# Two tables per pick with shared compares, and one-sample dot products on quarters of the array

## The chip, the cores and the metric

The kernel runs on one core of a Trainium2 chip. The time is device microseconds from one launch. TensorE multiplies matrices, VectorE (DVE) and ScalarE (ACT) work element by element, GpSimd (POOL) gathers rows of memory by index, and SyncE (SP) starts transfers.

## The reference

A recommendation tower for a batch of 512. Each sample has 32 ids, one per embedding table; each table has rows of 128 floats (1,000 to 125,000 rows). The 32 rows of a sample are multiplied with each other, and the products of different rows (496 of them), with 16 dense values, go through three dense layers.

```python
e = stack([tbl_f[ids[:, f]] for f in range(32)], axis=1)      # 512 x 32 x 128
z = einsum('bnd,bmd->bnm', e, e)[:, iu, ju]                   # pairs n < m: 512 x 496
h = concatenate([z, dense_ctx], axis=1)                       # 512 x 512
h = maximum(h @ W_top1 + b_top1, 0)                           # 512 x 512
h = maximum(h @ W_top2 + b_top2, 0)                           # 512 x 256
y = h @ W_top3                                                # 512 x 1
```

All of it is in 32-bit floats.

## The kernel before

All 32 rows of a sample are brought into `emb`, 128 partitions (the embedding's elements) x 512 samples x 32 tables. Seventeen tables are **gathered**: GpSimd starts 68 indirect transfers (line 307), each of 128 rows, paced by the picks that are done (`pace`), and TensorE transposes what lands (`turn`, line 574), one to four tiles at a time; ScalarE copies the transposed tiles into `emb` (`emb_out`).

The fifteen smallest tables are **picked**: they are loaded whole, and TensorE multiplies the table by a matrix of zeros and ones. A table has 8 or 10 row blocks (`KR`). Eleven tables of 1,000 rows have 8, four of 1,250 rows have 10, 128 blocks in all, taken in the order of their size. For each block:

- an `onehot` tile (128 x 512) is made by comparing the table's 512 ids, which every partition holds (`pick_id`, 16 bits), with the number of the row that the partition has in this block (`own_row`). VectorE makes some directly in 32 bits (`make_onehots`, line 326); for the others it writes 16 bits (`narrow`, line 336), and ScalarE widens them, several blocks in one instruction (line 442). `BY_ACT` says how many of a table's blocks go that second way, 75 in all.
- the table is split so that two fast passes give the full precision: ScalarE rounds it (`high`, line 421), VectorE subtracts (`low`, line 316). TensorE then does two matmuls per block (lines 564 and 566) with the same `onehot`.

Three tables, four tables' ids and 16 `onehot` tiles are held at a time. SyncE loads the ids and rows of the next table when the buffers come free. VectorE's order is written out: in the loop of table t it waits for the ids of table t+1 and makes its narrow compares, then makes the `low` pieces and direct compares of table t by turns. The ids of table t+1 were asked for when VectorE had finished table t-3, so they are there long before. TensorE does `pick(t)` and then `turn(t-2)`. A pair of tables shares one tile of PSUM, which ScalarE copies into `emb` when both are done (`pick_out`; the last three alone, `pick_alone`).

Then come the **dot products** (`dot_pairs`, line 606). One matmul takes two samples, 64 columns against themselves, and writes a 64 x 64 block, of which the two 32 x 32 blocks on the diagonal are used. Even and odd matmuls go to the two halves of the array's columns (`tile_position`). Eight groups of 64 samples follow each other; ScalarE and VectorE copy half a group each to SBUF (line 196), 512 columns of which a half is used later. The blocks are stored to memory and loaded back in another order (`dots_store`, `pairs_load`), and go through the three layers (lines 625, 636, 641). The order on TensorE after the picks is written out: dots of groups 0 to 5, the last transposes, group 6, layer 1 of the first half of the batch, the rest of the dots, layers 2 and 3.

Of the kernel before, what the change touches and what calls it, by code (L numbers as in the profile page):

```python
# [19 lines left out]

PIECE = 2
PIECES0 = KR[0] // PIECE
LOW_CUT, HOT_CUT = [4, 4, 2], [3]
# [8 lines left out]

LOWS = [cut(KR[0], [PIECE])] + [cut(k, LOW_CUT) for k in KR[1:]]
LOW0 = [sum(len(p) for p in LOWS[:t]) for t in range(PICK + 1)]

BY_ACT = [2, 4, 5, 5, 5, 5, 5, 5, 5, 5, 5, 6, 6, 6, 6]

HALF1 = KR[1] // 2

TWOS = -(-PICK // 2)  # L40
ACT0 = [sum(BY_ACT[:t]) for t in range(PICK + 1)]

ACT_K0 = [KR[t] - BY_ACT[t] if t < 3 else 0 for t in range(PICK)]
DVE_K0 = [0 if t < 3 else BY_ACT[t] for t in range(PICK)]
# [14 lines left out]
LAG = 2  # L59
TABLES_HELD, IDS_HELD, HOT, ROWS_HELD = 3, 4, 16, 7  # L60
# [4 lines left out]
def pace(c):  # L65
    return min(51 * c // 20 - 10, CHUNK0[PICK])
# [13 lines left out]
def build(nc, row_ids, pick_ids, tables, lone, picked, context, w1, w2, small, y):  # L80
# [4 lines left out]
    with ctx:  # L85
# [6 lines left out]
        def sem(name):  # L92
# [10 lines left out]
        pick_id = sb("pick_id", [P, IDS_HELD, B], i16)  # L103
        home = sb("home", [P, 2, 2 * F, BLK // 4], f32)
        table = home[:, :, :, :].rearrange("p i c g -> p (i c g)")[:, 0:TABLES_HELD * KRMAX * D].rearrange(
            "p (t n) -> p t n", t=TABLES_HELD)
        high = sb("high", [P, TABLES_HELD, KRMAX * D], f32r)
        low = sb("low", [P, TABLES_HELD, KRMAX * D], f32r)
        onehot = sb("onehot", [P, HOT, B], f32r)
        narrow = sb("narrow", [P, 2, NARROW, B], mybir.dt.float16)  # L110


        dot_sb = home
        pairs = sb("pairs", [P, BLOCKS, 4, PC, BLK // 4], f32)
        w1_sb = sb("w1_sb", [P, PC, H1], f32)
        w2_sb = sb("w2_sb", [P, N1, H2], f32)
        small_sb = sb("small_sb", [P, N1 + 2 * N2], f32)
        h1 = sb("h1", [P, N1, B], f32)
        h2 = sb("h2", [P, N2, B], f32)
        y_row = sb("y_row", [1, B], f32)  # L120
# [9 lines left out]
        pick_ps = [two_ps[(TWOS - 1) % 2][:, i, :] for i in range(2)]  # L130
        dot_ps = [free_ps, [two_ps[TWOS % 2][:, i, :] for i in range(2)]]
# [14 lines left out]
        pick_ids_in = [sem(f"pick_ids_in{t}") for t in range(PICK)]  # L146
# [16 lines left out]
        picked_done = sem("picked_done")  # L163
        pick_emb_ready = sem("pick_emb_ready")
        turned = sem("turned")
# [19 lines left out]
        def by_dve(t):  # L185

            return CHUNK0[t] - ACT0[t]
# [5 lines left out]
        def copy_dots(copy, grp, j):  # L193

            at = GRP // 4 * (grp % 2) + GRP // 8 * j
            return copy(dot_sb[:, grp // 2 % 2, :, at:at + GRP // 8],  # L196
                        dot_ps[grp % 2][j][:, :].rearrange("p (g c) -> p c g", c=2 * F))

        def dots_store(queue, r, s):
            queue.dma_start(dot_out[r][s, 0:F * F, :].rearrange("(a j) g -> a j g", j=F),  # L200
                            dot_sb[32 * s:32 * s + 32, r % 2, F * (s % 2):F * (s % 2) + F, :]
                            ).then_inc(dots_stored[r], 16)
# [18 lines left out]
        def copy_last_dots(copy, half):  # L221
# [3 lines left out]
                        last_dot_ps[half][:, 0:B // 2].rearrange("p (g c) -> p c g", c=2 * F))  # L225
# [4 lines left out]
        def _(sp):  # L230
            def ids_load(t):
                if t >= IDS_HELD:
                    sp.wait_ge(onehot_dve, by_dve(t - IDS_HELD + 1))
                    sp.wait_ge(narrow_ready, ACT0[t - IDS_HELD + 1])
                sp.dma_start(pick_id[:, t % IDS_HELD, :], pick_ids[:, t, :]).then_inc(pick_ids_in[t], 16)

            def table_load(t):
                if t >= TABLES_HELD:
                    sp.wait_ge(low_ready, LOW0[t - TABLES_HELD + 1])
                sp.dma_start(table[:, t % TABLES_HELD, 0:width(t)],  # L240
# [6 lines left out]
            for j in range(PIECES0):  # L247
                sp.dma_start(table[:, 0, n * j:n * (j + 1)], first[:, n * j:n * (j + 1)]).then_inc(piece_in[j], 16)
            table_load(1)
            for t in range(2, PICK):  # L250
                ids_load(t)
                table_load(t)
# [60 lines left out]
        def _(dve):  # L313
            def split_low(t, a, b):
                at = t % TABLES_HELD
                dve.tensor_tensor(low[:, at, a:b], table[:, at, a:b], high[:, at, a:b],  # L316
                                  ALU.subtract).then_inc(low_ready, 1)

            def make_onehots(t, k0, k1):

                i = STEPS.index(KR[t])
                for k in range(k0, k1):
                    c = CHUNK0[t] + k
                    if c >= HOT:
                        dve.wait_ge(picked_done, c - HOT + 1)
                    dve.tensor_scalar(onehot[:, c % HOT, :], pick_id[:, t % IDS_HELD, :], own_row[:, i, k:k + 1], None,  # L326
                                      ALU.is_equal).then_inc(onehot_dve, 1)

            def make_narrow(t):

                i = STEPS.index(KR[t])
                if t >= 2:
                    dve.wait_ge(onehot_act, ACT0[t - 1])
                for n in range(BY_ACT[t]):
                    k = ACT_K0[t] + n
# [442 lines left out]
```

## Time and profile before

| | |
|---|---|
| Time, three runs | 124.79, 125.47, 125.48 us (median 125.47) |
| Profiled execution: span from first to last instruction | 148.7 us |
| The profiled execution's own time beside the span | none is given but the span |
| Busy share of the span: TensorE, VectorE, ScalarE, GpSimd | 82%, 51%, 53%, 48% |
| Mean granted clock of TensorE | 0.919 |
| Picks (lines 564 and 566) | 4.8 to 79.4 us of the span |
| Dot products (line 606) | 83.8 to 131.4 us |

"Busy" is the time in which an engine had an instruction under way. The profiled execution is 23.2 us longer than the median of the runs, so its rows give durations, and their sum is not the time. A record of TensorE is one pass of instructions as the hardware has them: a product of 32-bit floats shows as more than one record.

### The profile page before, as it was taken

What the parts mean: (1) busy time and instruction counts of PE and PEld (TensorE: products, weight loads), DVE (VectorE), ACT (ScalarE), POOL (GpSimd) and SP (SyncE); (2) the same over time, 40 slices, a digit from 0 to 9 for tenths busy, and PEclk for the clock granted to TensorE, in tenths of its full rate; (3) what the DMA queues carried; (4) which work ended last, traced back from release to release, by engine and by line L of the source; (5) the groups of instructions that cost most, each with busy time, mean ns of one, the idle gap of its engine ahead of it and who ended that gap; (6) DMA issues with size and microseconds to landing.
All of it is one profiled execution on the core that took longest, in us unless ns stands there. A gap on an engine that the chain in (4) does not pass through costs nothing.

```text
span 148.7 us, 2677 instructions
## 1 busy us (share of the span) xinstructions
PE 121.4 (82%) x1028; PEld 99.5 (67%) x1028; DVE 75.2 (51%) x196; ACT 78.8 (53%) x79; POOL 71.3 (48%) x76
## 2 busy tenths in 40 slices
PE   5889979989999689499995464321999899999993
PEld 3457758868788468378884452111999798999971
DVE  2999999989897399496800000000333033223301
ACT  3588899999997897799950510000143302210022
POOL 3877749787787477378775577772000000000000
PEclk9999999999999999959999776555599999999999
DMA  5998736666667356793221011211056441024000
GB/s 144 275 338 267 234 100 204 204 216 225 217 219 235 110 178 195 232 324 113 55 53 52 23 53 53 53 53 35 4 146 202 136 126 35 4 78 127 10 0 1
DMA packets 11150, 19.81 MB, mean 133 GB/s; under 512 B 2353, under 2 KB 7473, under 8 KB 11138
## 3 DMA queue, kind: packets, MB, share of 16 engines
q1 hardware_dynamic: 7522, 13.74, 29.8%
q0 software_dynamic: 2176, 4.46, 10.3%
q10 hardware_dynamic: 1440, 1.44, 3.0%
q8 instruction: 8, 0.13, 0.3%
q14 instruction: 4, 0.03, 0.1%
HBM read 17.54 MB, written 2.13 MB: 132 GB/s over the span
## 4 chain that ended last, share of the span: by engine, by line
PE 64%; ACT 15%; issue 11%; another core or an unknown queue 5%; DVE 2%; DMA 2%; ACTq 0%
PE two_ps L564 15%; PE two_ps L566 14%; PE two_ps L606 8%; PE two_ps L625 8%; ACT onehot L442 8%; PE free_ps L606 7%; ACT emb L421 5%; PE free_ps L636 3%; PE turn_ps L574 3%; PE two_ps L636 2%; ACT high L421 2%; DMA id_sb<-row_ids 2%; PE two_ps L641 1%; PE turn_ps L625 1%
## 5 line engine op out<-in xcount | busy, mean ns | idle before, releaser
L307 POOL DMA_INDIRECT rows<-tables,row_no x64 | 66.6, 1040 | 26.5 <-issue 14.9
L564 PE MATMUL two_ps<-onehot,high 128*128 128x512 f32 x128 | 52.7, 412 | 7.4 <-ACT onehot L442 4.3
L566 PE MATMUL two_ps<-onehot,low 128*128 128x512 f32 x128 | 50.9, 397 | 0.0
L442 ACT ACTIVATE onehot<-narrow 128x2560 fp32r<-128x2560 f16 (+3 forms) x16 | 35.5, 2226 | 4.8 <-PE two_ps L566 3.0
L564 PEld LDWEIGHTS two_ps<-onehot,high 128*128 128x128 f32 x128 | 24.8, 193 | 16.7 <-issue 10.4
L566 PEld LDWEIGHTS two_ps<-onehot,low 128*128 128x128 f32 x128 | 24.8, 194 | 4.7
L326 DVE TENSOR_SCALAR onehot<-pick_id,own_row 128x512 fp32r<-128x512 int16 x53 | 23.0, 479 | 4.4 <-PE two_ps L566 3.5
L316 DVE TENSOR_TENSOR low<-home,high 128x512 fp32r<-128x512 f32 (+1 forms) x36 | 22.4, 625 | 3.8 <-issue 3.7
L336 DVE TENSOR_SCALAR narrow<-pick_id,own_row 128x512 f16<-128x512 int16 x75 | 22.4, 365 | 0.0
L606 PE MATMUL two_ps<-emb 128*64 128x64 f32 x240 | 12.9, 247 | 9.4 <-issue 9.3
L196 DVE COPY home<-free_ps 128x512 f32<-128x512 f32 x4 | 2.8, 692 | 33.8 <-remote 29.8
L421 ACT ACTIVATE high<-home 128x1024 fp32r<-128x1024 f32 (+3 forms) x19 | 17.8, 941 | 2.5 <-DMA home<-picked 2.4
L606 PEld LDWEIGHTS two_ps<-emb 128*64 128x64 f32 x240 | 10.3, 158 | 11.6 <-issue 11.5
L421 ACT ACTIVATE emb<-turn_ps 128x512 f32<-128x512 f32 (+2 forms) x20 | 11.3, 574 | 10.9 <-PE turn_ps L574 7.2
L606 PE MATMUL free_ps<-emb 128*64 128x64 f32 x272 | 11.7, 251 | 5.6 <-ACT emb L421 4.5
L421 ACT ACTIVATE emb<-two_ps 128x1024 f32<-128x1024 f32 (+1 forms) x9 | 12.8, 1421 | 6.4 <-remote 6.4
L606 PEld LDWEIGHTS free_ps<-emb 128*64 128x64 f32 x272 | 10.8, 164 | 6.7 <-ACT emb L421 5.2
L625 PE MATMUL two_ps<-pairs,w_sb 128*128 128x128 f32 x104 | 12.6, 277 | 0.0
L625 PEld LDWEIGHTS two_ps<-pairs,w_sb 128*128 128x128 f32 x104 | 12.0, 192 | 0.1
L421 ACT ACTIVATE home<-two_ps 128x512 f32<-128x512 f32 x4 | 2.4, 596 | 17.8 <-PE two_ps L606 17.8
L340 DVE TENSOR_SCALAR h<-two_ps,small_sb 128x128 f32<-128x128 f32 x15 | 4.3, 346 | 13.1 <-PE two_ps L625 12.2
L574 PE MATMUL turn_ps<-ident,rows 128*128 128x128 f32 x64 | 9.9, 274 | 0.8 <-issue 0.8
(37 smaller groups left out, 54.5 us busy)
## 6 DMA issues: line engine op xcount, KB each, us to landing
home<-picked SPq DMA_DIRECT2D x10, 512.0 KB, 3.6
home<-picked SPq DMA_DIRECT2D x4, 640.0 KB
pick_id<-pick_ids SPq DMA_DIRECT2D x13, 128.0 KB, 3.7
w_sb<-w SPq DMA_DIRECT2D x3, 512.0 KB
dot_out<-home SPq DMA_DIRECT2D x10, 128.0 KB, 2.4
rows<-tables,row_no POOLq DMA_INDIRECT x64
dot_out<-home ACTq DMA_DIRECT2D x6, 128.0 KB, 2.6
pairs<-dot_out SPq DMA_DIRECT2D x10, 64.0 KB, 2.0
```

The lines of the kernel that those rows point to most:

```text
L307: pool.indirect_dma_start(rows[:, k % ROWS_HELD, i, :], None, lone if one_table else tables, bass.IndirectOffsetOnAxis(ap=id_sb[:, 0, c:c ...
L316: dve.tensor_tensor(low[:, at, a:b], table[:, at, a:b], high[:, at, a:b], ALU.subtract).then_inc(low_ready, 1)
L326: dve.tensor_scalar(onehot[:, c % HOT, :], pick_id[:, t % IDS_HELD, :], own_row[:, i, k:k + 1], None, ALU.is_equal).then_inc(onehot_dve, 1)
L336: dve.tensor_scalar(narrow[:, t % 2, n, :], pick_id[:, t % IDS_HELD, :], own_row[:, i, k:k + 1], None, ALU.is_equal).then_inc(narrow_ready, 1)
L421: return act.activation(out, in_, ACT.Copy)
L442: act.activation(onehot[:, at:at + n, :], narrow[:, t % 2, n0:n0 + n, :], ACT.Copy).then_inc(onehot_act, n)
L564: pe.matmul(out, high[:, at, D * k:D * (k + 1)], onehot[:, c % HOT, :], start=(k == 0), stop=False)
L566: pe.matmul(out, low[:, at, D * k:D * (k + 1)], onehot[:, c % HOT, :], start=False, stop=(k == KR[t] - 1)).then_inc(picked_done, 1)
L574: last = pe.transpose(turn_ps[k % 2][:, i * P:(i + 1) * P], rows[:, k % ROWS_HELD, i, :], ident[:, :])
L606: last = pe.matmul(out, e, e, start=True, stop=True, tile_position=(0, 64 * h))
L625: last = pe.matmul(h1_ps[r][n], w1_sb[:, c, n * P:(n + 1) * P], pairs[:, r:r + 1, :, c, :], start=(c == 0), stop=(c == PC - 1))
L636: return pe.matmul(h2_ps[part][n], w2_sb[:, c, n * P:(n + 1) * P], h1[:, c, samples(part)], start=(c == 0), stop=(c == N1 - 1))
```

## The change

It does two things. **Teams.** Tables 1 to 14 are picked in seven teams of two tables of equal size; table 0 is alone (`TEAMS`). One compare serves the same row block of both tables, on 2 x 512 ids, because both have the same `own_row` number; `onehot` and `narrow` tiles have room for two tables. There are 68 such steps instead of 128 blocks, 25 of them by way of ScalarE (`BY_ACT`). Two teams are held (`HELD`), their rows, `high`, `low`, ids and `narrow` tiles, and 8 double `onehot` tiles. TensorE does a step of both tables, four matmuls, then the next; a team is cut in two halves with a `turn` behind each. In the last team the first table's steps from `SPLIT` on go ahead of the second's, so that it can be copied out earlier, and the copy of the second table is shared by ScalarE and VectorE. The weights of layer 2, the hidden layers and the result use the memory of the ids and `narrow` tiles, so that load waits for the last compares.

**Dots of one sample.** A matmul takes one sample, 32 columns against themselves, and goes to one of the four quarters of the array's columns in turn. All that is written is used; the copies to SBUF have half the columns.

```diff
+TEAMS = [[0]] + [[t, t + 1] for t in range(1, PICK, 2)]
+BY_ACT = [2, 3, 3, 3, 3, 3, 4, 4]
+HELD, HOT, ROWS_HELD = 2, 8, 7
 # SyncE
-                sp.wait_ge(onehot_dve, by_dve(t - IDS_HELD + 1))      # IDS_HELD = 4, tables
-                sp.wait_ge(narrow_ready, ACT0[t - IDS_HELD + 1])
+                sp.wait_ge(onehot_dve, DVE0[g - HELD + 1])            # HELD = 2, teams
+                sp.wait_ge(narrow_ready, ACT0[g - HELD + 1])
+                ids_load(sp, g)
+                table_load(g, 0)
+                table_load(g, 1)
...
+            sp.wait_ge(onehot_dve, DVE0[NT])
+            sp.wait_ge(narrow_ready, ACT0[NT])
             sp.dma_start(w2_sb[:, :, :], w2.rearrange("(c p) n -> p c n", p=P)).then_inc(weights_in, 16)
 # VectorE
+                    dve.tensor_scalar(onehot[:, c % HOT, 0:n, :], pick_ids_of[:, g % HELD, 0:n, :],
+                                      own_row[:, STEPS.index(KT[g]), k:k + 1], None,
                                       ALU.is_equal).then_inc(onehot_dve, 1)
...
+            for g in range(1, NT):
+                if 1 < g < NT - 1:
+                    dve.wait_ge(pick_ids_in[g + 1], 16)
+                    make_narrow(g + 1)
+                if g >= HELD:
+                    dve.wait_ge(picked_done, STEP0[g - HELD + 1])
+                own = KT[g] - BY_ACT[g]
+                pieces = [(i, k0, k1) for k0, k1 in LOWS[g] for i in range(2)]
+                for j, (i, k0, k1) in enumerate(pieces):
+                    if k0 == 0:
+                        dve.wait_ge(high_ready, PIECES0 + 2 * (g - 1) + i + 1)
+                    split_low(g, i, k0, k1)
+                    if j:
+                        n = len(pieces) - 1
+                        make_onehots(g, DVE_K0[g] + own * (j - 1) // n, DVE_K0[g] + own * j // n)
+                if g == 1:
+                    dve.wait_ge(pick_ids_in[2], 16)
+                    make_narrow(2)
+            dve.wait_ge(pick_emb_ready, NT + 1)
+            dve.tensor_copy(emb[:, BLK:B, F - 1], pick_ps[1][:, BLK:B]).then_inc(pick_emb_dve, 1)
 # TensorE
+            def row_block(g, i, k):
+                rows_of, hot = slice(D * k, D * (k + 1)), onehot[:, (STEP0[g] + k) % HOT, i, :]
+                out = two_ps[g % 2][:, i, :]
+                pe.matmul(out, high[:, g % HELD, i, rows_of], hot, start=(k == 0), stop=False)
+                return pe.matmul(out, low[:, g % HELD, i, rows_of], hot, start=False, stop=(k == KT[g] - 1))
...
             def dot_pairs(bank, b0, n):
                 for i in range(n):
-                    g, h = divmod(i, 2)
-                    e = emb[:, b0 + 2 * i:b0 + 2 * i + 2, :].rearrange("p b f -> p (b f)")
-                    out = bank[64 * h:64 * h + 64, 64 * g:64 * g + 64]
-                    last = pe.matmul(out, e, e, start=True, stop=True, tile_position=(0, 64 * h))
+                    g, h = divmod(i, 4)
+                    e = emb[:, b0 + i, :]
+                    out = bank[32 * h:32 * h + 32, 32 * g:32 * g + 32]
+                    last = pe.matmul(out, e, e, start=True, stop=True, tile_position=(0, 32 * h))
```

## Rows read from the trace of the kernel before

**Rows 1.** The page's first line.
```profile
span 148.7 us, 2677 instructions
```

**Rows 2.** The chain that ended last, by engine, shares of the span.
```profile
PE 64%; ACT 15%; issue 11%; another core or an unknown queue 5%; DVE 2%; DMA 2%; ACTq 0%
```

**Rows 3.** Stretches: busy us (records) PE, PEld, DVE, ACT, POOL; granted clock, DMA.
```profile
20.00:30.00 10.00, 10.00 (x49) 8.24 (x48) 9.91 (x28) 10.00 (x9) 7.00 (x6) 1.00 0.58 172
60.00:70.00 10.00, 7.75 (x30) 6.09 (x30) 7.45 (x19) 9.57 (x8) 5.99 (x7) 0.83 0.69 221
87.40:104.10 16.70, 5.47 (x32) 3.07 (x30) 0.00 (x0) 0.60 (x1) 10.52 (x12) 0.59 0.18 47
110.00:115.00 5.00, 5.00 (x163) 4.93 (x158) 1.74 (x3) 1.76 (x4) 0.00 (x0) 1.00 0.52 148
```

**Rows 4.** Order of time: start, us, instruction, count, idle before and its releaser.
```profile
50.95 0.47 PE L564 MATMUL two_ps<-onehot,high 128*128 128x512 f32 x1 [1.48 <-ACT onehot L442]
...
63.34 0.77 PE L564 MATMUL two_ps<-onehot,high 128*128 128x512 f32 x1 [2.25 <-ACT onehot L442]
...
82.75 1.02 ACT L421 ACTIVATE emb<-two_ps 128x512 f32<-128x512 f32 x1 [6.41 <-remote]
...
83.83 3.64 PE L606 MATMUL free_ps<-emb 128*64 128x64 f32 x61 [3.57 <-ACT emb L421]
...
104.13 2.51 PE L606 MATMUL two_ps<-emb 128*64 128x64 f32 x42 [0.94 <-issue]
```

**Rows 5.** Order of time: transposes, each behind a table's last row block.
```profile
18.19 0.27 PE L574 MATMUL turn_ps<-ident,rows 128*128 128x128 f32 x1
...
27.61 0.60 PE L574 MATMUL turn_ps<-ident,rows 128*128 128x128 f32 x4
...
31.70 0.60 PE L574 MATMUL turn_ps<-ident,rows 128*128 128x128 f32 x4
...
74.22 0.60 PE L574 MATMUL turn_ps<-ident,rows 128*128 128x128 f32 x4
...
79.22 1.04 PE L574 MATMUL turn_ps<-ident,rows 128*128 128x128 f32 x8
```

**Rows 6.** Order of time: VectorE's subtracts and compares.
```profile
7.12 0.74 DVE L316 TENSOR_TENSOR low<-home,high 128x256 fp32r<-128x256 f32 x2
...
18.56 0.68 DVE L316 TENSOR_TENSOR low<-home,high 128x512 fp32r<-128x512 f32 x1
19.16 1.27 DVE L326 TENSOR_SCALAR onehot<-pick_id,own_row 128x512 fp32r<-128x512 int16 x3
...
24.66 1.40 DVE L336 TENSOR_SCALAR narrow<-pick_id,own_row 128x512 f16<-128x512 int16 x5
...
35.69 0.48 DVE L326 TENSOR_SCALAR onehot<-pick_id,own_row 128x512 fp32r<-128x512 int16 x1
...
54.07 0.34 DVE L336 TENSOR_SCALAR narrow<-pick_id,own_row 128x512 f16<-128x512 int16 x1
```

**Rows 7.** Order of time: ScalarE's rounding and widening.
```profile
8.04 1.16 ACT L421 ACTIVATE high<-home 128x512 fp32r<-128x512 f32 x2
...
11.63 1.04 ACT L421 ACTIVATE high<-home 128x1024 fp32r<-128x1024 f32 x1
...
33.85 2.40 ACT L442 ACTIVATE onehot<-narrow 128x2560 fp32r<-128x2560 f16 x1
```

**Rows 8.** Transfers: an issue in time; tables by size, us to landing; ids.
```profile
7.89 0.33 SPq L240 DMA_DIRECT2D home<-picked  x1
...
home<-picked SPq DMA_DIRECT2D x10, 512.0 KB, 3.6
...
DMA to landing us min/median/max: 2.6/3.1/3.7
```

**Rows 9.** Order of time: dot products, and products of layer 1.
```profile
110.66 2.08 PE L606 MATMUL free_ps<-emb 128*64 128x64 f32 x64
...
112.53 2.08 PE L606 MATMUL two_ps<-emb 128*64 128x64 f32 x64
...
117.08 7.41 PE L625 MATMUL two_ps<-pairs,w_sb 128*128 128x128 f32 x64
```

More of the change, by code:

```diff
@@ L19 @@
 STEPS = sorted(set(KR))
+TEAMS = [[0]] + [[t, t + 1] for t in range(1, PICK, 2)]
+NT = len(TEAMS)
+KT = [KR[team[0]] for team in TEAMS]
+assert PICK % 2 and all(KR[t] == KT[g] for g, team in enumerate(TEAMS) for t in team)
+STEP0 = [sum(KT[:g]) for g in range(NT + 1)]
 PIECE = 2
 PIECES0 = KR[0] // PIECE
-LOW_CUT, HOT_CUT = [4, 4, 2], [3]
+LOW_CUT = [4, 4, 2]
 def cut(k, sizes):
@@ L30, in cut @@
     return list(zip(at[:-1], at[1:]))
[L33 to L44, printed above, removed]
+LOWS = [cut(KT[0], [PIECE])] + [cut(k, LOW_CUT) for k in KT[1:]]
+LOW0 = [sum(len(p) * len(team) for p, team in zip(LOWS[:g], TEAMS[:g])) for g in range(NT + 1)]
+BY_ACT = [2, 3, 3, 3, 3, 3, 4, 4]
+ACT0 = [sum(BY_ACT[:g]) for g in range(NT + 1)]
+DVE0 = [STEP0[g] - ACT0[g] for g in range(NT + 1)]
+ACT_K0 = [KT[g] - BY_ACT[g] if g < 2 else 0 for g in range(NT)]
+DVE_K0 = [0 if g < 2 else BY_ACT[g] for g in range(NT)]
+SPLIT = 6
 GRP, BLK = 64, 128
@@ L145, in build @@
         row_ids_in = sem("row_ids_in")
-        pick_ids_in = [sem(f"pick_ids_in{t}") for t in range(PICK)]
+        pick_ids_in = [sem(f"pick_ids_in{g}") for g in range(NT)]
         piece_in = [sem(f"piece_in{j}") for j in range(PIECES0)]
@@ L247, in _ @@
             for j in range(PIECES0):
[L248 to L252, printed above, removed]
+                sp.dma_start(table[:, 0, 0, n * j:n * (j + 1)], first[:, n * j:n * (j + 1)]).then_inc(piece_in[j], 16)
+            table_load(1, 0)
+            table_load(1, 1)
+            for g in range(2, NT):
+                sp.wait_ge(onehot_dve, DVE0[g - HELD + 1])
[3 more added lines that the diff above has]
+                table_load(g, 1)
             for r in range(BLOCKS):
@@ L648, in _ @@
                           start=True, stop=True)
-            for t in range(PICK):
-                pick(t)
-                if t >= LAG:
-                    turn(t - LAG)
+            pick(0, 0, KT[0])
+            for g in range(1, NT - 1):
+                if g >= 2:
+                    pe.wait_ge(pick_emb_ready, g - 1)
+                pick(g, 0, KT[g] // 2)
+                if g >= 2:
+                    turn(2 * g - 3)
+                pick(g, KT[g] // 2, KT[g])
+                turn(2 * g - 2)
+            g = NT - 1
+            pe.wait_ge(pick_emb_ready, g - 1)
+            pick(g, 0, KT[g] // 2)
+            turn(2 * g - 3)
+            pick(g, KT[g] // 2, SPLIT)
+            for k in range(SPLIT, KT[g]):
+                step_waits(g, k)
+                last = row_block(g, 0, k)
+            last.then_inc(picked_first, 1)
+            for k in range(SPLIT, KT[g]):
+                row_block(g, 1, k).then_inc(picked_done, 1)
+            turn(2 * g - 2)
             turn(TURNED - 1)
-            pe.wait_ge(pick_emb_ready, TWOS + 1)
+            pe.wait_ge(pick_emb_ready, NT + 1)
             dot_group(0)
@@ L657, in _ @@
             dot_group(1)
+            pe.wait_ge(pick_emb_dve, 1)
             dot_group(2)
```

229 lines of the change are left out of this document (102 added, 127 removed).

## The prediction

> **What bounds the kernel now.** I read the page's head and the slices first, then the chain of waits, then the stretches, then the order of time around every idle spell of TensorE. The span is 148.7 us [rows 1] against a median of 125.47 us for the timed runs, so before any step is priced one must know what those 23.2 us are. The chain gives TensorE 64%, and 11% to "issue", time in which nothing visible was waited for [rows 2]. The stretches put that in one place: from 87.4 to 104.1 TensorE starts 32 matmuls in 16.7 us, while from 110 to 115 it starts 163 in 5 us, of the same two loops [rows 3]. In the order of time there are three such spells [rows 4]: 1.5 us before 50.95, 2.25 us before 63.34 (with a granted clock of 0.83 from 60 to 70 [rows 3], so 1.7 us more), and the long one: ScalarE gets word of the last pick, started at about 79, only at 82.75, and the dot products begun at 83.83 crawl until 104.13. The reader is to see that the wait is for nothing the program orders. From 79.4 to 104.1, 24.7 us, the work is a 1.0 us copy, some 90 records of 29 ns and four transposes of 0.11 us, 4.1 us in all; 20.6 us are lost there, 1.3 us more at half the clock behind it (42 records in 2.51 us), and 5.5 us in the two spells before. I take all 27.4 us as disturbance of this one execution: the three timed runs lie within 0.7 us of each other, and could not hold even the largest of them. What remains, 121.3 us, stands 4.2 us under the median; that is what lies around the span, and I add the differences below to the median.
>
> So read, the kernel is two stages. **Picks**: from 20 to 30 us TensorE is busy all the time, and so are VectorE (9.9 of 10) and ScalarE (10.0) [rows 3]; three engines are level. From transpose group to transpose group a table of 8 row blocks takes 4.09 us, one of 10 takes 5.00 [rows 5]. Without the spells the picks end at 79.2 - 1.5 - 2.3 - 1.7 = 73.8 us. **Dots and layers**: from 105 on TensorE has no idle time to speak of [rows 3], so a microsecond of pick time moves the end by a microsecond.
>
> **The picks, part by part.** TensorE does the same 256 matmuls and the same transposes, so a team of two tables of 8 cannot take it under 2 x 4.09 = 8.2 us, one of 10 not under 10.0.
>
> VectorE: a compare on 512 ids is followed 0.40 us later by the next (three in 1.27, the last 0.48) where it writes 32 bits, 0.265 us later (five in 1.40, the last 0.34) where it writes 16; a subtract of 512 takes 0.60 (18.56 to 19.16), of 256 0.33 (two in 0.74, the last 0.41) [rows 6]. What doubling a compare to 1,024 ids costs is not in the trace. Bounds: twice a single one (0.80 and 0.53, nothing shared), or less by a fixed part. The subtracts give that as 2 x 0.33 - 0.60 = 0.06. The two compares read the same ids and differ by 0.135; if the part that grows with the ids halves with the written size it is 0.27 and 0.135, and the fixed part 0.13. I take the latter, being from the instruction in question: 0.66 and 0.40. A team of 8 then costs VectorE 3 narrow (1.2) + 4 subtracts (2.4) + 5 direct (3.3) = 6.9 us, where two tables now cost 2 x 3.7; a team of 10, 1.6 + 3.1 + 4.0 = 8.7. ScalarE widens 3,072 elements per team where it widened 2 x 2,560 (2.40 us each) [rows 7]: some 1.9 us less per pair of tables. It stops being level with TensorE, which buys nothing unless VectorE keeps up.
>
> **The wait that is added.** Only two teams' ids are held, where four tables' were. SyncE loads the ids of team g once VectorE has made the last direct compare of team g-2, the last thing in VectorE's loop of that team. The first thing VectorE does in the next loop, of team g-1, is to wait for exactly those ids, for the narrow compares of g. Nothing stands between, so the whole way of a transfer is VectorE's idle time, and behind it in VectorE's order stand the subtracts and compares that TensorE needs next. Its price: SyncE starts 0.03 us after the release (7.86 to 7.89); 128 KB of ids landed in 2.6 us at best, a table of 512 KB in 3.6 [rows 8]; the new load has 256 KB and goes ahead of its tables. Between 2.6 and 3.6 I take 2.8, with the tail of the compare 2.9 us. It is paid in the loops of teams 2 to 6. The team loop is then 2.9 + 6.9 = 9.8 us (8) and 11.6 (10) for VectorE, against 8.2 and 10.0 for TensorE: VectorE sets the pace.
>
> The sequence: VectorE has the first table done at 7.86 [rows 6] and ScalarE starts the second table's rounding at 8.04 [rows 7]. Three narrow compares, two roundings of 1.0 (both tables are needed for the first step), two subtracts and a compare bring team 1's first step to about 11.4; two more subtracts and four compares end VectorE's loop at 15.2, TensorE's last four steps follow, and the team ends at 19.3, where now the third table ends at 18.2 [rows 5]. Loop 2 ends at 15.2 + 2.9 + 1.2 + 5.7 = 25.0, loop 3 at 34.8, loop 4 at 44.6, loop 5 (narrow compares for a team of 10) at 54.8, with its first two subtracts at 50.3, so TensorE does team 5 from 50.3 to 58.5. In loop 6 the ids and narrow compares end at 59.3 and the first subtracts at 60.5, so TensorE stands 2.0 us. Teams 6 and 7 (9.7 and 9.6, now TensorE's pace) end at 79.8. The picks lose 79.8 - 73.8 = 6.0 us.
>
> Other moves around it: after the last pick the wait for a 1.0 us copy becomes the wait for two groups of transposes, 0.9, since half of that copy goes to VectorE: -0.1. The second layer's weights load behind the last compare, with some 20 us of layer 1 and dots to hide it. The gathers are paced by steps done, and move with the picks.
>
> **The dot products.** One product is two records now: 32 products are the 64 records in 1.87 us (112.53 less 110.66), 29.2 ns each [rows 9]. A record of 128 columns on the whole array starts 113 ns after the one before (64 in 7.41 us, the last lasting about 0.28); a 64-column record would take 57 by that, and 29 shows two running side by side on the array's halves, 58.4 each. On the line through 113 ns at 128 columns and 58.4 at 64, a 32-column record takes 31.1 ns alone. The change has 512 products, so 1,024 records. Bounds: four abreast, 1,024 x 7.8 = 8.0 us against 15.0 now, -7.0; none faster than today's pace, 1,024 x 29.2 = 29.9 us, +15.0. I take a value between, from the order of issue: a sample's two records use the same quarter, so the second waits for the first, and the next sample's first stands behind it in the queue. At any time a second record and the next first one overlap, two, never four. That is 1,024 x 15.55 = 15.9 us, +0.9. Today's pace scales with the clock (61 records in 3.64 us at half of it, some 57 ns each [rows 4]), which says the array sets it today, not the issue. The Trainium skill (TensorEngine Tiling (Array Packing), Theoretical Speedup) promises up to 4x for a dimension of at most 32, which would be the first bound. The half-width copies behind the dots lie beside TensorE's work and gain nothing.
>
> **Sum**: +6.0 - 0.1 + 0.9 = +6.8, 132.3 us.
>
> **Rivals.** (1) *The ids come in time and the picks run at TensorE's pace.* It decides when a load lands within 8.2 - 6.9 = 1.3 us of the last compare, or VectorE's wide work is that much cheaper. Then team 2 starts at 19.3, four teams take 8.2 and the two of 10 end at 71.4: -2.4 in the picks, -1.6 in all, 123.9. For it: three level engines now, and VectorE and ScalarE both relieved. Against: the quickest load of half the ids took 2.6 us [rows 8]. (2) *Four abreast*: +5.9 - 7.0, 124.4. For it: quarters are independent; against: the pairs of records in one queue. (3) *Issue becomes the bound of the dots*: twice the instructions at no better pace than the rows show, +5.9 + 15.0, 146.4. For it: no stretch of the trace has a faster one; against: the pace halved with the clock. The Trainium skill (TensorE: Matmul & The Clock Gate, "Wait — 56ns, not 53.3ns?") says starts never come closer than about 25 ns; by that 25.6 us, about 142, and no row here has a closer mean. (4) *The shared compare shares nothing*: 0.13 x 8 to 10 per team, about +6 on VectorE's path, 138.
>
> **Numbers.** Forecast (with picks between +3 and +9 for a load of 2.3 to 3.5 us) 0.49, (1) 0.19, (2) 0.11, (3) 0.13, (4) 0.08. Within 1% (1.25 us, about what a measurement tells from no change), above 124.2, fall 0.06 of (2), 0.06 of (1) and 0.01 of the forecast, should the load cost far less than I take: 0.13. Faster is the rest of (1) and (2), 0.18; slower is what remains, 0.69. The range leaves out (3) and the upper side of (4): 123 to 139; the forecast's own is 128 to 136.
>
> **What would show it.** VectorE idle some 2.5 us before each first narrow compare of teams 3 to 7, ended by the ids' DMA; TensorE idle 1 to 2 us ahead of each team, ended by a subtract. Were the narrow compares back to back with the direct ones, (1) holds. 128 dot records in 2.0 us show the order argument right, in 1.0 (2), in 3.7 (3). Wide compares at 0.66 and 0.40 apart show (4) wrong. The forecast fails if VectorE's loop is under 8.2 us, or TensorE's dots leave 15 us by more than 2.

## The result, and the profile after

The changed kernel takes 141.24 us (median of four runs, 139.86 to 141.33) where the kernel before took 125.31 beside it: a ratio of 1.128 (95% interval 1.120 to 1.135), 15.9 us slower. The forecast of 132.3 us had the sign and missed the size, and the time lies above the range of 123 to 139.

The first rows are the page's: span, granted clock in 40 slices, the queue that brings instruction blocks (transfers, MB, share), and the chain that ended last, by engine, which answers to [rows 2]; "issue" has 12% of it here too, this time with a cause in the program.

```profile
span 139.3 us, 3584 instructions
...
PEclk9999999996899995999999999955555699999999
...
q8 instruction: 12, 0.20, 0.5%
...
PE 70%; issue 12%; DMA 6%; ACT 5%; DVE 4%; SPq 2%; ACTq 0%
```

This execution took 141.15 us itself, so 1.85 us lie around its span. The kernel before, profiled once more without the spells of [rows 4], took 125.15 us with this span and queue:

```profile
span 123.3 us, 2677 instructions
...
q8 instruction: 8, 0.13, 0.4%
```

That profile stands in for the one of [rows 1] below; I call it the quiet one. Three stretches of the changed kernel are below full clock: two of 3.4 us in the picks (within 32 to 36 and 52 to 56 us), and one from 90 to 110, where the dot products are.

**The picks after.** VectorE in order of time (start, us, instruction, count, idle before and its releaser): the narrow compares of teams 4 to 6, where the kernel before had none of these waits [rows 6], and some direct ones between.

```profile
29.98 1.28 DVE L353 TENSOR_SCALAR late<-pick_id,own_row 128x1024 f16<-128x1024 int16 x3 [4.09 <-DMA pick_id<-pick_ids]
...
32.38 0.75 DVE L343 TENSOR_SCALAR onehot<-pick_id,own_row 128x1024 fp32r<-128x1024 int16 x1
...
33.64 1.41 DVE L343 TENSOR_SCALAR onehot<-pick_id,own_row 128x1024 fp32r<-128x1024 int16 x2
...
39.66 1.28 DVE L353 TENSOR_SCALAR late<-pick_id,own_row 128x1024 f16<-128x1024 int16 x3 [2.67 <-DMA pick_id<-pick_ids]
...
49.50 1.67 DVE L353 TENSOR_SCALAR late<-pick_id,own_row 128x1024 f16<-128x1024 int16 x4 [2.77 <-DMA pick_id<-pick_ids]
```

The ids' transfers in the list of DMA issues (count, KB, median us to landing), for those of half the size in [rows 8]:

```profile
pick_id<-pick_ids SPq DMA_DIRECT2D x6, 256.0 KB, 2.8
```

TensorE in order of time, with what it waits for ahead of a team, and the transposes behind the last pick, which answer to [rows 5]:

```profile
21.38 0.47 PE L579 MATMUL two_ps<-onehot,high 128*128 128x512 f32 x1 [1.05 <-DVE low L334]
...
32.56 0.76 PE L579 MATMUL two_ps<-onehot,high 128*128 128x512 f32 x1 [2.74 <-issue]
...
82.44 1.03 PE L594 MATMUL turn_ps<-ident,rows 128*128 128x128 f32 x8
```

The reader is to see the same wait in every loop. From one group of narrow compares to the next it is 9.7 and 9.8 us in these rows (11.2 us in the loop before them, which ends with the wait of 4.09, and 10.25 in the one behind, of a team of 10). TensorE is starved by 1.0 to 2.7 us ahead of three teams. "Issue" at 32.56 only says that no releaser was matched; such stands go when the ids come in time (below).

**The dot products after**, TensorE in order of time, up to layer 1 and behind it, for [rows 9]:

```profile
83.41 1.67 PE L626 MATMUL free_ps<-emb 128*32 128x32 f32 x128
85.01 0.66 PE L594 MATMUL turn_ps<-ident,rows 128*128 128x128 f32 x4
85.59 0.39 PE L626 MATMUL two_ps<-emb 128*32 128x32 f32 x23
86.90 1.35 PE L626 MATMUL two_ps<-emb 128*32 128x32 f32 x105 [0.92 <-issue]
88.10 0.62 PE L626 MATMUL free_ps<-emb 128*32 128x32 f32 x23
90.75 1.79 PE L626 MATMUL free_ps<-emb 128*32 128x32 f32 x105 [2.02 <-issue]
92.32 0.76 PE L626 MATMUL two_ps<-emb 128*32 128x32 f32 x22
95.10 1.87 PE L626 MATMUL two_ps<-emb 128*32 128x32 f32 x106 [2.03 <-issue]
...
107.69 8.79 PE L645 MATMUL two_ps<-pairs,w_sb 128*128 128x128 f32 x64
116.32 1.04 PE L594 MATMUL turn_ps<-ident,rows 128*128 128x128 f32 x8
117.61 0.76 PE L626 MATMUL free_ps<-emb 128*32 128x32 f32 x64 [0.25 <-ACT emb L437]
118.22 0.75 PE L626 MATMUL two_ps<-emb 128*32 128x32 f32 x64
```

Two more such stands follow, 1.52 and 2.00 us: five before layer 1, 8.5 us in sum. From the end of one stand to the start of the next, TensorE does 105 + 23, 105 + 22, 106 + 21 and 107 + 20 records, 127 or 128, whatever group or bank they belong to. A record has its weight load, so that is 256 instructions. The extra 1,024 instructions of the dots (1,024 records in place of 512, a load with each) are four blocks more on the instruction queue, 12 for 8, and 0.20 - 0.13 = 0.07 MB: 256 instructions to a block. The totals fit too: 2 x 1,028 matmuls and loads before are 8.0 times 256, 2 x 1,540 after are 12.0 times. In the trace such blocks leave at 88.02, 92.64, 96.33 and 100.61 us, and the bursts begin at 90.75, 95.10, 98.78 and 103.02, 2.4 to 2.7 us later each time. Each of these blocks left only 1.1 to 1.9 us after the burst before it had begun (at 86.90, 90.75, 95.10 and 98.78), so most of its way lay behind that burst. The same holds beyond this kernel: seven profiles of this case have such stands among their dot products, and all 27 of over 0.5 us for which no releaser is seen end 2.2 to 2.7 us after a block has left. Where long work stands between the groups, as behind layer 1 at 117.61, there is no stand, and 64 records take 0.61 us (118.22 - 117.61), 9.5 ns each.

For comparison, the quiet profile of before, same view:

```profile
75.37 1.04 PE L574 MATMUL turn_ps<-ident,rows 128*128 128x128 f32 x8
76.68 2.08 PE L606 MATMUL free_ps<-emb 128*64 128x64 f32 x64 [0.27 <-ACT emb L421]
...
91.30 3.84 PE L625 MATMUL two_ps<-pairs,w_sb 128*128 128x128 f32 x32
...
99.00 1.04 PE L574 MATMUL turn_ps<-ident,rows 128*128 128x128 f32 x8
```

Where the 16.0 us between the two spans went, from these rows:

| stretch | before (quiet) | after | difference |
|---|---|---|---|
| to the transposes behind the last pick | 75.37 | 82.44 | +7.07 |
| to the first dot product | 1.31 | 0.97 | -0.34 |
| dot products up to layer 1 | 14.62 | 24.28 | +9.66 |
| layer 1, first two blocks | 7.70 | 8.63 | +0.93 |
| the rest | 24.30 | 22.98 | -1.32 |

The stretches (us, busy us and records of PE, PEld, DVE, ACT, POOL, granted clock, DMA) show why layer 1 is longer: its beginning falls at half clock (granted 0.5, the 1.2 GHz level), to which TensorE had fallen at 90.1 us, during the second of the stands, while the work itself is the same. First the changed kernel:

```profile
83.40:107.70 24.30, 15.08 (x843) 13.24 (x842) 3.07 (x7) 4.64 (x11) 14.02 (x15) 0.64 0.45 120
...
107.69:116.32 8.63, 8.63 (x72) 8.63 (x65) 1.13 (x4) 0.38 (x1) 0.00 (x0) 0.83 0.26 71
```

and the quiet one of before, where TensorE is busy 13.9 of 14.6 us, at full clock:

```profile
76.70:91.30 14.60, 13.91 (x426) 13.30 (x426) 4.15 (x6) 5.43 (x11) 11.22 (x12) 1.00 0.52 148
```

### The profile page after: what moved, and what is told of

Read it like the earlier page. It is cut to its first block, busy times and chain, and to the rows that moved or that the text cites. A ratio compares the mean times of both kernels' runs of the same rounds, so it can differ in the third digit from the quotient of the medians.

```text
span 139.3 us, 3584 instructions
## 1 busy us (share of the span) xinstructions
PE 116.6 (84%) x1540; PEld 95.5 (69%) x1540; DVE 68.4 (49%) x137; ACT 63.7 (46%) x70; POOL 72.9 (52%) x76
## 4 chain that ended last, share of the span: by engine, by line
PE 70%; issue 12%; DMA 6%; ACT 5%; DVE 4%; SPq 2%; ACTq 0%
PE two_ps L579 18%; PE two_ps L580 17%; PE two_ps L645 10%; PE free_ps L626 6%; PE turn_ps L594 5%; PE two_ps L626 5%; DMA home<-picked 4%; PE free_ps L656 3%; ACT onehot L457 3%; PE two_ps L656 2%; DVE onehot L343 2%; DMA pick_id<-pick_ids 2%; DVE low L334 2%; PE two_ps L661 2%; PE turn_ps L645 1%
## 5 line engine op out<-in xcount | busy, mean ns | idle before, releaser
L325 POOL DMA_INDIRECT rows<-tables,row_no x64 | 68.1, 1065 | 25.1 <-issue 13.7
L579 PEld LDWEIGHTS two_ps<-onehot,high 128*128 128x128 f32 x128 | 25.1, 196 | 18.9 <-issue 7.5
L343 DVE TENSOR_SCALAR onehot<-pick_id,own_row 128x1024 fp32r<-128x1024 int16 (+1 forms) x43 | 29.5, 716 | 0.2
L580 PEld LDWEIGHTS two_ps<-onehot,low 128*128 128x128 f32 x128 | 25.2, 197 | 4.9
L457 ACT ACTIVATE onehot<-late 128x3072 fp32r<-128x3072 f16 (+2 forms) x8 | 22.2, 2773 | 6.7 <-PE two_ps L580 6.3
L437 ACT ACTIVATE high<-home 128x1024 fp32r<-128x1024 f32 (+2 forms) x18 | 17.3, 964 | 14.0 <-DMA home<-picked 12.3
L353 DVE TENSOR_SCALAR late<-pick_id,own_row 128x1024 f16<-128x1024 int16 (+1 forms) x25 | 10.4, 470 | 13.9 <-DMA pick_id<-pick_ids 13.9
L645 PEld LDWEIGHTS two_ps<-pairs,w_sb 128*128 128x128 f32 x104 | 13.4, 210 | 0.3 <-issue 0.2
L626 PE MATMUL free_ps<-emb 128*32 128x32 f32 x544 | 8.8, 223 | 4.5 <-issue 3.5
L626 PE MATMUL two_ps<-emb 128*32 128x32 f32 x480 | 7.8, 222 | 4.9 <-issue 4.9
L626 PEld LDWEIGHTS free_ps<-emb 128*32 128x32 f32 x544 | 7.6, 134 | 6.0 <-issue 4.1
L437 ACT ACTIVATE emb<-two_ps 128x1024 f32<-128x1024 f32 (+2 forms) x9 | 9.5, 1055 | 2.8 <-PE two_ps L580 2.8
L626 PEld LDWEIGHTS two_ps<-emb 128*32 128x32 f32 x480 | 6.8, 133 | 5.8 <-issue 5.5
L594 PEld LDWEIGHTS turn_ps<-ident,rows 128*128 128x128 f32 x64 | 8.1, 146 | 1.5
```

The costliest lines, as they stand in the source:

```text
L325: pool.indirect_dma_start(rows[:, k % ROWS_HELD, i, :], None, lone if one_table else tables, bass.IndirectOffsetOnAxis(ap=id_sb[:, 0, c:c ...
L343: dve.tensor_scalar(onehot[:, c % HOT, 0:n, :], pick_ids_of[:, g % HELD, 0:n, :], own_row[:, STEPS.index(KT[g]), k:k + 1], None, ALU.is_eq ...
L353: dve.tensor_scalar(narrow[:, g % HELD, j, 0:n, :], pick_ids_of[:, g % HELD, 0:n, :], own_row[:, STEPS.index(KT[g]), k:k + 1], None, ALU.i ...
L437: return act.activation(out, in_, ACT.Copy)
L457: act.activation(onehot[:, at:at + n, 0:nt, :], narrow[:, g % HELD, n0:n0 + n, 0:nt, :], ACT.Copy).then_inc(onehot_act, n)
L579: pe.matmul(out, high[:, g % HELD, i, rows_of], hot, start=(k == 0), stop=False)
```

## The experiments

My theory after the comparison: two losses that add up, the late ids in the picks and the supply of instructions in the dots. The rivals: one of the two is all of it, or the dots are slow from the array, the clock or the groups.

**The kernel before, again.** No edit.

> The kernel before, unchanged, profiled again, because its first profiled execution was disturbed and the prediction rests on a pick end of 73.8 us and a span of 121.3 us that were worked out by taking the disturbance away. If that working was right, a quiet profile shows the last pick at about 73.8 us and a span of about 121.3 us. The rival: only about 1.8 us lie around the span, as in the changed kernel's profile (139.3 us of span in an execution of 141.15 us), and then the quiet span is about 123.5 us and the picks end at about 75 to 76 us.

Measured: 125.15 us, span 123.3, last pick done at 75.4. The rival holds: 1.85 us lie around the span, where I had 4.2, and the picks end 1.6 us later than I worked out. That 121.3 + 4.2 makes 125.5 is no confirmation, since the 4.2 us were what was left to the median. The start of the forecast, the median, does not suffer from this, but its loss of the picks does: it was counted from 73.8 us, and from 75.4 it would have been 79.8 - 75.4 = 4.4 us in place of 6.0.

**Teams alone.** The changed kernel with the products of 64 columns:

```diff
-                    g, h = divmod(i, 4)
-                    e = emb[:, b0 + i, :]
-                    out = bank[32 * h:32 * h + 32, 32 * g:32 * g + 32]
+                    g, h = divmod(i, 2)
+                    e = emb[:, b0 + 2 * i:b0 + 2 * i + 2, :].rearrange("p b f -> p (b f)")
+                    out = bank[64 * h:64 * h + 64, 64 * g:64 * g + 64]
```

> Picks in teams as in the changed kernel, dot products of two samples on 64 columns as in the kernel before. Theory 1 (two separate losses: the late ids in the picks, the instruction supply in the dots): the picks end near 82 us as in the changed kernel and the dots run as in the kernel before, so 131 to 133 us, +6 to +8 on the kernel before. Rival (the picks are the whole loss, and the dots are only slow because a clock spoiled by the picks slows them): 138 to 141 us. Rival (the dots are the whole loss, since a late pick end is taken up by the gathers): 125 to 127 us.

Measured: 132.18 us, ratio 1.063 (1.052 to 1.073), +6.9. VectorE's waits for ids in the view of waits (us, times, longest), and the transposes behind the last pick:

```profile
DVE late L353 <- DMA pick_id<-pick_ids: 13.3, 5, 3.0
```
```profile
81.85 1.03 PE L594 MATMUL turn_ps<-ident,rows 128*128 128x128 f32 x8
```

The picks end 6.5 us later than in the quiet profile (81.85 - 75.37), and no more than that is lost to the end (span 129.6 against 123.3). Theory 1 holds.

**Narrow dots alone.** The kernel before with the opposite edit, run twice:

> Picks as in the kernel before, dot products of one sample on 32 columns as in the changed kernel. Theory 1 (instruction supply: a block of 256 TensorE instructions arrives every 4.1 us, and 2,048 instructions of the dots need eight of them): 133 to 136 us, bursts of about 1.8 us with stands of 2 us between them at about 32 ns for each product record. Rival (the array itself takes the records two abreast at 15 to 17 ns): 124 to 126 us. Rival (four abreast at about 8 ns, and the stands in the changed kernel came from the teams' late start): 118 to 121 us.

Measured: 134.62 us, 132.11 to 135.30, too scattered for an interval. So again:

> The kernel with the narrow dots alone a second time, for an interval, since its first four runs lay between 132.1 and 135.3 us. Theory 1 (two separate losses that add up: 132.2 with the teams alone, 141.2 with both): 133.5 to 135.5 us, a ratio of 1.065 to 1.08. Rival (the two losses share a part): 131 to 133 us.

Measured: 135.01 us, ratio 1.080 (1.073 to 1.087). In the second one's order of time, picks as before and stands as in the changed kernel:

```profile
75.65 1.03 PE L574 MATMUL turn_ps<-ident,rows 128*128 128x128 f32 x8
76.95 1.73 PE L606 MATMUL free_ps<-emb 128*32 128x32 f32 x128 [0.27 <-ACT emb L421]
...
83.79 1.73 PE L606 MATMUL free_ps<-emb 128*32 128x32 f32 x113 [1.48 <-issue]
...
88.81 1.98 PE L606 MATMUL two_ps<-emb 128*32 128x32 f32 x113 [3.13 <-issue]
...
102.08 7.41 PE L625 MATMUL two_ps<-pairs,w_sb 128*128 128x128 f32 x64
```

25.1 us from the first product to layer 1 (102.08 - 76.95), with a span of 132.8. The two losses, 6.3 and 9.5 us of span, make 15.8 of the 16.0. They add up; neither two abreast nor four abreast tells the time of the dots.

**Ids ahead.** The changed kernel with the ids of four teams, in the place of the later `pairs`; the second layer's weights get a place of their own:

```diff
+        pick_id = pairs[:, :, :, :, :].rearrange("p r s c g -> p (r s c g)").bitcast(i16)
+        pick_ids_of = pick_id.rearrange("p (g t b) -> p g t b", g=IDS_HELD, t=2)
...
-                ids_load(sp, g)
+                if g + 1 < NT:
+                    if g + 1 >= IDS_HELD:
+                        sp.wait_ge(onehot_dve, DVE0[g + 1 - IDS_HELD + 1])
+                        sp.wait_ge(narrow_ready, ACT0[g + 1 - IDS_HELD + 1])
+                    ids_load(sp, g + 1)
```

> The changed kernel with the ids of four teams held instead of two: they lie where the pair sums go later, and the ids of a team are requested one team earlier. Theory 1 (the exposed 2.9 us load of ids ahead of the narrow compares sets the pace of the picks): the waits of 2.7 to 4.1 us for ids go, the picks keep TensorE's pace and end at 74 to 76 us, and the time is 133 to 135 us. Rival (VectorE is the pace even with ids in time, through the release of the onehot blocks): the idle time only changes its name, picks end at 80 to 82 us, 139 to 141 us.

Measured: 134.40 us, ratio 1.080 (1.069 to 1.091) to the kernel before, 6.8 less than the changed one. VectorE has the ids (now in `pairs`) in time, and its loop of a team of 8 takes 6.98 us (32.07 - 25.09). VectorE, then TensorE, in order of time:

```profile
25.09 1.27 DVE L353 TENSOR_SCALAR late<-pairs,own_row 128x1024 f16<-128x1024 int16 x3
...
32.07 1.27 DVE L353 TENSOR_SCALAR late<-pairs,own_row 128x1024 f16<-128x1024 int16 x3
```
```profile
73.64 1.03 PE L594 MATMUL turn_ps<-ident,rows 128*128 128x128 f32 x8
...
78.47 0.66 PE L594 MATMUL turn_ps<-ident,rows 128*128 128x128 f32 x4 [1.83 <-DMA rows<-tables,row_no]
```

So the exposed load was the loss of the picks, and without it the shared compares bring their end 1.7 us ahead of the kernel before, at TensorE's pace. The last row is a new wait, for gathered rows.

**Twice the columns, as many instructions.** The kernel before, each product cut into two on neighbouring quarters, moving the same 64 columns:

```diff
-                    out = bank[64 * h:64 * h + 64, 64 * g:64 * g + 64]
-                    last = pe.matmul(out, e, e, start=True, stop=True, tile_position=(0, 64 * h))
+                    for q in (2 * h, 2 * h + 1):
+                        last = pe.matmul(bank[32 * q:32 * q + 32, 64 * g:64 * g + 64], emb[:, b0 + 2 * i + q % 2, :], e,
+                                         start=True, stop=True, tile_position=(0, 32 * q))
```

> The kernel before, with each product of 64 by 64 columns cut into two with 32 stationary columns on neighbouring quarters of the array, each moving the same 64 columns: as many products as in the changed kernel (512), each moving twice the columns. Theory 1 (a block of 256 instructions every 4.1 us is the bound, whatever the array does): bursts longer, stands shorter, the sum unchanged, 133 to 136 us as with the dots of 32 columns alone (134.6). Rival (the array is the bound and the stands have a cause that follows each block of work, not of instructions): the bursts of 1.7 us double and the stands stay at 2 us, so dots 8 to 13 us longer than with 32 columns, 142 to 148 us.

Measured: 134.43 us, ratio 1.075 (1.069 to 1.081), as with half the columns. In order of time, and its stretch:

```profile
88.16 1.84 PE L606 MATMUL two_ps<-emb 128*32 128x64 f32 x113 [0.98 <-issue]
...
92.06 2.10 PE L606 MATMUL free_ps<-emb 128*32 128x64 f32 x115 [1.66 <-issue]
...
96.42 2.03 PE L606 MATMUL two_ps<-emb 128*32 128x64 f32 x116 [2.05 <-issue]
```
```profile
88.00:101.70 13.70, 8.63 (x440) 7.46 (x440) 2.08 (x3) 2.95 (x6) 9.44 (x10) 1.00 0.60 166
```

The stands come at full clock too (1.00 in this stretch), so the half clock elsewhere is not their cause. Nor does their pace change with it: here bursts begin 3.9 and 4.4 us apart, and 3.7 to 4.4 us in the changed kernel at half clock. 113 of these records of 64 columns start within 1.66 us (the next ones at 89.82), 14.7 ns each, half of the 29.2 of [rows 9]: with quarters the array does 64 columns twice as fast, and the time is not better. Against a plain reading: this stage, 25.2 us like the one above, contains 2.3 us of waiting for gathered rows, during which blocks could arrive, and 3.4 us at half clock before the rows shown; its four stands are 5.2 us in sum.

**Half the instructions, by bfloat16.** The narrow dots alone, from rounded embeddings:

```diff
-        emb = sb("emb", [P, B, F], f32)
+        emb = sb("emb", [P, B, F], mybir.dt.bfloat16)
```

> The kernel before with the dot products of one sample on 32 columns, from embeddings rounded to bfloat16 (so the products are less exact): one record with its weight load for each of the 512 products instead of two, 1,024 instructions as in the kernel before instead of 2,048. Theory 1 (instruction supply): four blocks instead of eight, so the loss of 9.4 us goes: 122 to 126 us, still with stands between bursts of 256 instructions, because the array is done with each block early. Rival (the stands come from changing the quarter with each product, or are one for every 64 products): eight stands of 2 us stay, 130 to 134 us.

Measured: 135.21 us (133.67 to 135.94). My forecast for the time was wrong, from a cost that I had not counted: ScalarE's copies of the picks into `emb`, in the view of that line (min, median, max ns), first bfloat16, then the quiet profile:

```profile
L421 ACT ACTIVATE emb<-two_ps x9: 2469/2601/4635, 19.3 to 83.8; 128x1024 bf16<-128x1024 f32 x6, 128x512 bf16<-128x512 f32 x3
```
```profile
L421 ACT ACTIVATE emb<-two_ps x9: 1057/1215/2088, 20.2 to 75.6; 128x1024 f32<-128x1024 f32 x6, 128x512 f32<-128x512 f32 x3
```

Writing 2-byte elements, one or two at a stride of 64 bytes, took 2.6 us on the median where 4-byte ones at 128 took 1.2. The nine copies take 25.5 us in sum where they took 13.1, on an engine that is level with TensorE in the picks, and the dots begin at 86.33 in place of 76.68. The stage itself, up to layer 1 at 100.85, takes 14.5 us against 25.1, with two stands before its transposes, so of the theory only the part on the dots held.

**Half the products.** The same question without that cost: of the 64 products of a group only 32 are made, and the copies take their results twice.

```diff
-                for i in range(n):
+                for i in range(n // 2):
```

> The kernel with the narrow dots alone, with every second half of a group's products left out (256 products of 32 columns in place of 512; the others' results stand twice), so 1,024 instructions instead of 2,048 and as many groups, hand-overs and copies as before. Theory 1 (a stand for every 256 instructions): half of the stands go, the stage from the first product to layer 1 is 14 to 16 us against 24.6 us with all the products, time 123 to 126 us. Rival (a stand with each group, from changing banks or the hand-over to the copies): the stands stay and only the bursts halve, the stage is 20 to 21 us, 130 to 132 us.

Measured: 123.00 us, ratio 0.980 (0.971 to 0.988); the stage takes 13.4 us (77.22 to 90.62), with two stands:

```profile
80.88 0.64 PE L608 MATMUL free_ps<-emb 128*32 128x32 f32 x49 [1.29 <-issue]
...
85.61 0.91 PE L608 MATMUL free_ps<-emb 128*32 128x32 f32 x50 [2.55 <-issue]
```

Stands again about 128 records apart, now in every second group: they go with instructions, not with groups, banks or hand-overs. The stage is a little under the 14 to 16 us of theory 1, the time in its range (of half the dots, so no gain).

**Both losses undone.** Ids ahead, and products of 64 columns:

> Teams with the ids of four teams held, and the dot products of 64 columns as in the kernel before: both losses undone, the shared compares kept. Theory 1: the picks end 1.7 us earlier than in the kernel before (73.6 against 75.4 us in the profiles), but GpSimd issues its gathers back to back at 1.25 us each until about 97 us in either kernel, so most of the 1.7 us is waited for again in the transposes: 123.5 to 125.5 us, within 1.5% of the kernel before. Rival (the gathers have slack, the gain of the picks goes through to the end): 122.5 to 123.5 us. Rival (something else of the teams costs after the picks): 126 us and more.

Measured: 125.24 us, ratio 0.997 (0.992 to 1.001), no difference. The picks end about 1 us ahead (74.40 against 75.37), and it is given back to the gathers: the next transposes wait for gathered rows and start at 78.59, against 78.69. GpSimd by line (busy us, mean ns, idle before) in the quiet profile and in this kernel, and this kernel's TensorE in order of time:

```profile
L307 POOL DMA_INDIRECT rows<-tables,row_no x64 | 65.9, 1030 | 20.8 <-PE two_ps L566 11.0 <-issue 9.8
```
```profile
L325 POOL DMA_INDIRECT rows<-tables,row_no x64 | 68.9, 1076 | 19.5 <-issue 15.8 <-PE two_ps L580 3.7
```
```profile
78.59 0.66 PE L594 MATMUL turn_ps<-ident,rows 128*128 128x128 f32 x4 [1.15 <-DMA rows<-tables,row_no]
```

GpSimd spends 3 us more on the same 64 gathers and issues the last one 2.3 us later (96.35 against 94.08), back to back at the end in both, so an earlier end of the picks only lengthens the wait. That the teams make the gathers longer is not shown: with the picks of the kernel before they took 1,136 ns on the mean in the run with twice the columns, and 1,074 in the second one below. What makes them differ was not tried.

**Narrow products where layer 1 covers them.** As the last one, and then the kernel before, with products of 32 columns for the last 128 samples only:

```diff
+                if grp // 2 == LAST:
+                    dot_singles(dot_ps[grp % 2][j], GRP * grp + GRP // 2 * j, GRP // 2)
+                else:
+                    dot_pairs(dot_ps[grp % 2][j], GRP * grp + GRP // 2 * j, GRP // 4)
```

> As the one before, with the products of 32 columns in the last block of 128 samples only, where layer 1's long products stand between the groups. Theory 1 (an instruction block costs nothing where long work runs while it is fetched): the four last groups are each 0.35 us shorter without a stand, as in the kernel with the narrow dots alone (from its last eight transposes to its end 23.2 us against 24.3), so about 1 us less than the one before: 122.5 to 124.5 us. Rival (the supply is lost there too): stands of 1 to 2 us in the last groups, equal to the one before or up to 3 us slower.

> The kernel before, with the products of 32 columns in the last block of 128 samples only. Theory 1 (the supply costs nothing where layer 1 runs between the groups): the last four groups and their halves are 1.1 to 1.4 us shorter in sum, 123.8 to 124.6 us, and as fast as the same tail on the teams with early ids (124.64), because the gathers set the end of the teams' gain. Rival (the gain of 0.5% measured there was the teams'): no difference from the kernel before, 125.0 to 125.5 us.

Measured: 124.64 us on the teams, ratio 0.995 (0.990 to 0.999), and 124.47 us on the kernel before, 0.993 (0.989 to 0.996). In the latter's order of time there is no stand, and 64 records take 0.61 us where the quiet profile has 0.98 from 100.29 to 101.27 for 32 of 64 columns:

```profile
100.11 0.76 PE L613 MATMUL free_ps<-emb 128*32 128x32 f32 x64 [0.25 <-ACT emb L425]
100.72 0.81 PE L613 MATMUL two_ps<-emb 128*32 128x32 f32 x64
```

Both lie half a per cent or a little more under the kernel before, a small gain that the interval of the first barely clears. That the simpler one does as well says that the tail is the gain; none from the teams is seen.

## Why the prediction was wrong

**What bounds the kernel: right in the main.** The quiet profile has none of the long spells of [rows 4], so they were disturbance. But too much was taken out: the span is 123.3 us, not 121.3, and the picks end at 75.4, not 73.8. The reading that the wait was "for nothing the program orders" went too far for the short spells, whose releaser in [rows 4] is ScalarE's `onehot`: the quiet profile has five such waits, 2.9 us in sum, one of 0.44 us at the place of the 1.48.

**The picks: right in mechanism, and in size partly by luck.** Predicted +6.0; the teams alone measured 6.5 us at the end of the picks, the changed kernel 7.07. Both ends that the 6.0 is the difference of were put too early, by 1.6 us before (73.8 for 75.4) and by 2.1 with the teams alone (79.8 for 81.85, of which 1.1 us was there at the first of the waiting loops), and the two errors nearly cancel. The wait stands where it was put, 13.9 us in five waits of 1.5 to 4.1, 2.8 on the mean, against 2.9 predicted. The estimate for the wide compares held: three narrow ones in 1.28 us, two direct ones in 1.41 with the last lasting 0.75, so 0.40 and 0.66 apart, and a loop of 9.7 to 9.8 us with the wait and 6.98 without, for 9.8 and 6.9. The changed kernel's picks end 0.6 us behind those of the teams alone, where no wait is over 3.0 us and the clock is full throughout. It has the wait of 4.09 us and the two stretches at half clock; which of them costs how much is not shown.

**The copy after the last pick**: -0.34 for -0.1.

**The dots: this step failed.** I took +0.9 "from the order of issue: a sample's two records use the same quarter, so the second waits for the first", 15.55 ns a record, and set the floor aside because "today's pace scales with the clock (...), which says the array sets it today, not the issue". Both halves were wrong. Where nothing holds them, the records take 9.5 ns each, better than two abreast. And that the array sets the pace today does not say how far below it the next limit lies: TensorE came to the end of its instructions. The runs show what the time follows: the number of instructions (half of them, 13.4 us; all, 25.1) and hardly the columns (twice as many, 25.2). That the wait is for the transfer of the next block is inferred, from the stands' spacing of 256 instructions, the four extra transfers, and their start 2.2 to 2.7 us ahead of each burst in seven profiles; no run here could change the transfer by itself. In the kernel before, a block of 64-column records lasts 128 x 29.2 ns = 3.7 us, longer than these 2.2 to 2.7, and no stand is seen.

The sign that the prediction named for this step was too narrow as well: the first 128 records take 1.60 us (83.41 to 85.01), between its marks of 1.0 and 2.0, and say nothing of the stands behind them. Its wider sign, dots that leave 15 us by more than 2, did show the miss (24.28 us up to layer 1 alone).

The Trainium skill (Runtime: NRT & Kernel Launch, Instruction fetch mechanics) says that an engine's instructions come in blocks of 256, the next one fetched while the current one is executed, and that crossing a block is "mostly hidden". The block's size agrees with the rows (four more blocks for 1,024 more instructions). That it is hidden does not: here stands of 0.9 to 2.0 us a block are not. By that page's rule the stage's 832 records would have taken 832 x 9.5 ns = 7.9 us where 416 took 12.1 (at 29.2 ns), 4.2 us less than before, and it took 9.66 more.

**Rival (3), issue as the bound of the dots**, given 0.13, is what happened in kind. Its price of +15.0 assumed a floor of 29.2 ns for all 1,024 records. The first 832 ran at just that mean (24.28 us / 832 = 29.2 ns), by coincidence of bursts and stands; the last 192 lie behind layer 1's long products, where their blocks had time to arrive, and gained 1.3 us. With layer 1's half clock the dots lost 9.66 + 0.93 - 1.32 = 9.3 us. Rivals (1) and (4) were settled as forecast: the ids do not come in time, and the compare shares its fixed part. (2) was nearly right of the array, 9.5 ns a record where nothing holds them for its 7.8, and its time fell with the supply.

**What was missed in the rows**: the page of the kernel before counts its instruction blocks, and the dots' own share could have been worked out (512 records and as many loads, four blocks in 15 us). Doubling the instructions of a stage that should get shorter was the question to ask.

## What to carry to other kernels

Before cutting matmuls into smaller ones, count instructions per microsecond, not columns: in these runs bursts of short matmuls came to a stand every 256 instructions, and gained only where longer work stood between them. When buffers are counted in larger units (two teams for four tables), ask of each load how long after its release its first reader comes; here the answer was "at once", and one load's whole way was paid in every loop. And look which engine is second: the picks' gain, once had, was waited for again in the gathers.

## What the runs showed of the hardware that was not expected

- Matmul records of 32 columns on rotating quarters took 9.5 ns each (64 in 0.61 us), of 64 columns on quarters 14.7 ns, against 29.2 ns for 64 columns on halves, all at full clock. The Trainium skill (TensorE: Matmul & The Clock Gate, "Wait — 56ns, not 53.3ns?"), which the prediction named beside its rival (3), says that starts never come closer than about 25 ns. On rotating column groups they did, and the measurement decides.
- Instruction blocks for TensorE took 0.9 to 1.5 us each in the traces, and a burst began 2.2 to 2.7 us after its block's transfer had.
- ScalarE's copies from PSUM to a strided bfloat16 tile took 2.6 us (median of nine) where the same copies to 4 bytes took 1.2.
- GpSimd's gathers took 1,065 to 1,085 ns on the mean beside the wide compares, and 1,030 to 1,136 beside the narrower ones, so the compares are not shown to be the cause.
